# Last stage of a graph-recurrent layer: sums and squares of a block spread over the slots of the blocks before it, lower weights taken from PSUM, PSUM copies on ScalarE

## The reference, cut to what matters

```
xr = h.reshape(b, t * n * d)
mu = xr.mean(axis=0); var = xr.var(axis=0)
xr = (xr - mu) / jnp.sqrt(var + 1e-05) * bn_gamma + bn_beta
h = xr.reshape(b, t, n, d)
lmu = h.mean(axis=(1, 2, 3)); lvar = h.var(axis=(1, 2, 3))      # per row
h = (h - lmu) / jnp.sqrt(lvar + 1e-05) * ln_gamma + ln_beta
scores = jnp.squeeze(h @ attn_w.T + attn_b, -1)
w = jax.nn.softmax(scores, axis=-1)
out = jnp.einsum('btn,btnd->btd', w, h)
```

## Time and profile before

| | us |
|---|---|
| median of 3 runs | 2437.35 (2435.56 to 2440.09) |
| the profiled execution | 2435.1 |
| its span in the trace | 2433.3 |
| TensorE busy in the span | 2279.1 (94%) |
| VectorE, ScalarE, GpSimd busy | 1103.7, 975.1, 135.1 |

### The profile page before, as it was taken

How to read it: one execution, slowest core, us unless ns; L and a number is a source line. 1 busy time by engine, 2 the same in 40 slices (tenths; PEclk the granted TensorE clock), 3 DMA queues, 4 the chain that set the end, 5 groups by cost and what they waited for, 6 DMA issues and landing times. The chain is left out here.

```text
span 2433.3 us, 35457 instructions
## 1 busy us (share of the span) xinstructions
PE 2279.1 (94%) x12462; PEld 1815.6 (75%) x12462; DVE 1103.7 (45%) x2191; ACT 975.1 (40%) x1625; POOL 135.1 (6%) x124
## 2 busy tenths in 40 slices
PE   8999999999999999999999993999999999957787
PEld 7888888888888888888888882887878777832333
DVE  5333223233244332223333222677778777764456
ACT  4322212222233222122222121777778777746340
POOL 0000000000000000000000000111111101004230
PEclk9999999999999999999999996999999999977899
DMA  6321122221253220222220213445455454338430
GB/s 225 122 84 48 69 84 88 88 84 39 75 178 119 85 89 28 86 88 85 87 86 28 88 29 107 129 141 149 142 146 153 139 152 135 111 105 204 128 93 5
DMA packets 137744, 250.97 MB, mean 103 GB/s; under 512 B 11734, under 2 KB 97398, under 8 KB 134390
## 3 DMA queue, kind: packets, MB, share of 16 engines
q1 hardware_dynamic: 119546, 212.59, 28.5%
q10 hardware_dynamic: 18144, 37.69, 4.8%
HBM read 182.54 MB, written 67.70 MB: 103 GB/s over the span
## 5 line engine op out<-in xcount | busy, mean ns | idle before, releaser
L344 PE MATMUL psum<-w_hi,x_lo 128*128 128x500 f32 x2080 | 821.0, 395 | 8.2 <-DVE w_lo L214 8.2
L344 PE MATMUL psum<-w_lo,x_hi 128*128 128x500 f32 (+1 forms) x2080 | 810.3, 390 | 0.0
L344 PE MATMUL psum<-w_hi,x_hi 128*128 128x500 f32 x1920 | 746.1, 389 | 0.0
L278 DVE TENSOR_REDUCE rows<-u 128x10 f32<-128x500 f32 x160 | 107.6, 673 | 919.3 <-ACT u L227 919.1
L344 PEld LDWEIGHTS psum<-w_hi,x_lo 128*128 128x128 f32 x2080 | 391.6, 188 | 83.7 <-issue 8.2
L344 PEld LDWEIGHTS psum<-w_lo,x_hi 128*128 128x128 f32 (+1 forms) x2080 | 392.2, 189 | 75.3
L344 PEld LDWEIGHTS psum<-w_hi,x_hi 128*128 128x128 f32 x1920 | 360.9, 188 | 73.4
L233 ACT COPY at<-psum 128x640 f32<-128x640 f32 x160 | 111.0, 693 | 699.8 <-PE psum L324 699.8
L679 PE MATMUL psum<-adj_sb,xs_sb 100*64 100x100 f32 x2048 | 239.7, 391 | 29.6 <-DMA xs_sb<-xm 29.6
L679 PEld LDWEIGHTS psum<-adj_sb,xs_sb 100*64 100x64 f32 x2048 | 197.8, 219 | 64.3 <-issue 64.3
L227 ACT ACTIVATE u<-psum 128x500 f32<-128x500 f32 x160 | 94.0, 587 | 334.2 <-PE psum L344 334.2
(11 more groups left out here) (162 smaller groups left out, 2319.6 us busy)
## 6 DMA issues: line engine op xcount, KB each, us to landing
w_raw<-W SPq DMA_DIRECT2D x140, 500.0 KB, 6.8
adjT<-at SPq DMA_DIRECT2D x320, 125.0 KB
adj_sb<-adjT SPq DMA_DIRECT2D x16, 2500.0 KB
hF<-hC ACTq DMA_DIRECT2D x96, 256.0 KB, 2.2
h<-hF SPq DMA_DIRECT2D x64, 256.0 KB, 4.6
xs_sb<-xm SPq DMA_DIRECT2D x32, 400.0 KB
xg_sb<-xg ACTq DMA_DIRECT2D x14, 800.0 KB, 13.4
h<-hF SPq DMA_DIRECT2D x48, 192.0 KB, 3.8
```

The source lines that it names most:

```text
L278: nc.vector.tensor_reduce(rows[:, 0], u[:, c2], AX.X, ALU.add).then_inc(dve_step, 1)
L344: last = nc.tensor.matmul(mm_out(w % 2), a[0:r, k, cols], b[0:r, k, :], start=k == 0 and n == 0, stop=k == KF and n == 1)
```

## The change

- `sums_of` of block `i + 1` stands one batch to a slot. Batches 0 to 3 (`EARLY`) of block `i + 2` stand in slots 3 to 6 of block `i`, batches 4 to 6 of block `i + 1` in slots 0 to 2. Ahead of block 0 stand all of block 0 and four batches of block 1. The matmul of `acc` gets its own function, `close_sums`, at the end of slot 2, and `turn_sums` follows the spreads of slot 3.
- The turn of the next block's first weights comes ahead of the last pool batch and of `finish`; the other two kinds are turned in slot 1 instead of slot 0.
- `w_lo` is made from PSUM instead of from `wT`, so it waits for `w_hi` alone; ScalarE copies `wT` 0 later.
- The copies `qs`, `O_sb` and `res` go from VectorE to ScalarE, whose order is written anew.
- `sq` and `sqp` have four buffers instead of three.
- VectorE's woven softmax begins behind the first chunk of slot 3.

The same matmuls, squares, additions and DMAs are made as before.

```diff
+SQ_BUFS = 4
...
-        ahead = lambda i: (5 if i == 0 else 1) if i + 1 < NBLK else 0
-        SUMS_AT = 2
-        POOL_FIRST = batches[SUMS_AT][-1]
+        EARLY = 4
+        POOL_FIRST = batches[QC - EARLY][0]
...
 # VectorE
             def softmax(i):
-                dve.wait_ge(sums_done, i + 1)
-                wait(dve, qt_done, i)
-                V.tensor_copy(qs[:], q_bank).then_inc(qs_ready, 1)
-                yield
                 dve.wait_ge(qt_done, i + 1)
...
-                if i:
-                    result(i - 1)
-                dve.wait_ge(wT_ready, 3 * i + 1)
-                V.tensor_tensor(w_lo[:], wT[:, 0], w_hi[:].bitcast(fp32), ALU.subtract).then_inc(w_lo_ready, 1)
...
-                dve.wait_ge(pr_used, FC * (i + 1))
-                V.tensor_copy(O_sb[:], o_bank).then_inc(o_ready, 1)
...
+            def low_weights(i):
+                dve.wait_ge(w_hi_ready, i + 1)
+                V.tensor_tensor(w_lo[:], wT_bank(0), w_hi[:].bitcast(fp32), ALU.subtract).then_inc(w_lo_ready, 1)
...
             for i in range(NBLK):
+                low_weights(i)
                 pool(i)
-            result(NBLK - 1)
...
 # ScalarE
+            def softmax(i):
+                copy_sums(i)
+                squares(i + 1, 0, 1)
                 act.wait_ge(var_ready, i + 1)
                 nc.scalar.activation(st[:, 7], st[:, 6], ACT.Sqrt, bias=eps[:]).then_inc(rstd_ready, 1)
-                for k in range(first // 2):
-                    square(i + 1, k)
+                squares(i + 1, 2)
                 act.wait_ge(shifted, i + 1)
                 nc.scalar.activation(sc[:, 2, :, 0:TN], sc[:, 1, :, 0:TN], ACT.Exp).then_inc(exp_ready, 1)
-                for k in range(first // 2, first):
-                    square(i + 1, k)
-                copy_weights(i)
+                squares(i + 1, 3)
+                high_weights(i)
+
+            squares(0, *range(QC))
+            softmax(0)
+            for i in range(NBLK):
+                if i:
+                    result(i - 1)
+                copy_weights(i, 0)
+                squares(i + 1, EARLY)
+                copy_weights(i, 1, 2)
+                squares(i + 1, *range(EARLY + 1, QC))
                 if i + 1 < NBLK:
-                    for k in range(first, FC):
-                        square(i + 1, k)
+                    softmax(i + 1)
+                copy_pooled(i)
+            result(NBLK - 1)
...
 # TensorE
+            close_sums(0)
             turn_sums(0)
+            for n in range(EARLY):
+                sums_of(1, n)
+            pe.wait_ge(cols_ready, 2)
+            turn_weights(0, 0)
             for i in range(NBLK):
-                left = list(range(QC)) if i + 1 < NBLK else []
-                while left and left[0] < ahead(i):
-                    sums_of(i + 1, left.pop(0))
-                if i == 0:
-                    pe.wait_ge(cols_ready, 2)
-                turn_weights(i, 0)
                 pe.wait_ge(w_lo_ready, i + 1)
                 for n in range(QC):
                     spread_weights(i, n)
-                    if n == 0:
+                    if n == 1:
                         turn_weights(i, 1)
                         turn_weights(i, 2)
-                    for _ in range(2):
-                        if left:
-                            sums_of(i + 1, left.pop(0))
+                    if n == QC - EARLY and i + 1 < NBLK:
+                        turn_sums(i + 1)
+                    if n < QC - EARLY:
+                        if i + 1 < NBLK:
+                            sums_of(i + 1, EARLY + n)
+                    elif i + 2 < NBLK:
+                        sums_of(i + 2, n - (QC - EARLY))
                     if n:
                         for k in batches[n - 1]:
                             pool_chunk(i, k)
-                    if n == SUMS_AT and i + 1 < NBLK:
-                        assert not left
-                        turn_sums(i + 1)
+                    if n == QC - EARLY - 1 and i + 1 < NBLK:
+                        close_sums(i + 1)
+                if i + 1 < NBLK:
+                    turn_weights(i + 1, 0)
                 for k in batches[QC - 1]:
                     pool_chunk(i, k)
                 finish(i)
```

More of the change, by code:

```diff
@@ L1067, in square, with squares @@
                     g = i * len(on_pool) + on_pool.index(k)
-                    wait(act, sqp_used, g - 2)
-                    nc.scalar.activation(sqp[:, g % 3], h[:, i % 2, c, :], ACT.Square, bias=Csq[:, c:c + 1],
+                    wait(act, sqp_used, g - SQ_BUFS + 1)
+                    nc.scalar.activation(sqp[:, g % SQ_BUFS], h[:, i % 2, c, :], ACT.Square, bias=Csq[:, c:c + 1],
                                          scale=A[:, c:c + 1]).then_inc(sqp_ready, 1)
-            def copy_weights(i):
-                for k in range(3):
+            def squares(i, *which):
+                for n in which if i < NBLK else ():
+                    for k in batches[n]:
+                        square(i, k)
@@ L1075, in copy_weights, with copy_sums, high_weights @@
+            def copy_sums(i):
+                act.wait_ge(sums_done, i + 1)
+                wait(act, qt_done, i)
+                nc.scalar.copy(qs[:], q_bank).then_inc(qs_ready, 1)
+            def high_weights(i):
+                act.wait_ge(wT_done, 3 * i + 1)
+                wait(act, wb_done, FC * i)
+                nc.scalar.copy(w_hi[:], wT_bank(0)).then_inc(w_hi_ready, 1)
+            def copy_weights(i, *which):
+                for k in which:
                     act.wait_ge(wT_done, 3 * i + k + 1)
@@ L1076, in copy_weights, with copy_pooled @@
                     if k == 0:
-                        wait(act, wb_done, FC * i)
-                        wait(act, w_lo_ready, i)
+                        act.wait_ge(w_lo_ready, i + 1)
                         wait(act, res_done, i)
-                        nc.scalar.copy(w_hi[:], wT_bank(k))
                     nc.scalar.copy(wT[:, k], wT_bank(k)).then_inc(wT_ready, 1)
-            for k in range(FC):
-                square(0, k)
-            for i in range(NBLK):
-                first = sum(len(batches[n]) for n in range(ahead(i)))
+            def copy_pooled(i):
+                act.wait_ge(pr_used, FC * (i + 1))
+                wait(act, res_done, i)
+                nc.scalar.copy(O_sb[:], o_bank).then_inc(o_ready, 1)
```

30 lines of the change are left out of this document (15 added, 15 removed).

## The result

| | before | changed |
|---|---|---|
| median of 4 runs each | 2436.45 (2435.05 to 2440.09) | 2406.11 (2400.33 to 2409.12) |
| ratio | 1 | 0.9869, 95% interval 0.985 to 0.9887 |
| profiled execution | 2435.1 | 2409.12 |
| its span | 2433.3 | 2407.3 |

The forecast was 2405. The program is 30.3 us faster by the medians, 26.0 by the two profiled executions. To see where, I cut stage 3 at its first square, its first spread, and the end of each block's result matmuls.

A forecast was written before the change was run, and what follows sets the result against it. Bound: engines taking turns, none full. Gains 7.5 (opening) - 0.2 + 9.3 + 11.9 (blocks 0 to 2) + 2.5 (block 3) = 31.0 us, giving 2404.1 from the profiled execution, 2406.4 from the median; forecast 2405, range 2394 to 2418.

The forecast's parts named there:

- the meetings: Softmax of blocks 0 and 1: GpSimd adds hold up VectorE steps, two to three times a block, 2.0 us.
- Opening: First square to first spread: sums 2.3 us earlier, exponential 2.8, turn of weights 7.0, `w_lo` 0.5; together 7.5 us gained.
- Small parts: Fourth buffer worth 2.3 us in the opening, `w_lo` from PSUM 0.5 us a seam, copies nothing; about 4 us.
- `qs` cost the same on ScalarE: Copies `O_sb`, `res` and `qs` in the blocks: moving them from VectorE changes their cost by at most 0.1 us.
- Block 0: 45.4 us plus 1.4 for first spreads at TensorE's lower level, less 0.5: 46.3 us, 0.2 more than before.
- Blocks 1 and 2: Thinner sums and a shorter seam: 45.4 and 42.8 us instead of 54.74 each, gaining 9.3 and 11.9.
- VectorE's chain of 17.7 less one `pr` is 17.0: Later half of a block, slots 3 to 6: VectorE's work sets the time, 17.0 us, with TensorE's 15.8 hidden.
- rival (a): Blocks 0 to 2: the 2.5 us of waits in slots 0 and 1 vanish, 7.5 less, 2397 us; 18%.
- Rival (b): Softmax of blocks 0 and 1: seven adds each hold a VectorE step 1.04 us, 7.3 a block, 2416 us; 22%.
- Exponential: Later half of a block: it waits 0.6 us behind twelve squares, a square root and two table loads on ScalarE.
- (c): Slots 3 to 6: ScalarE, TensorE and VectorE still take turns, blocks 0 to 2 save nothing, 2425 us; 4%.
- (d): Four blocks: TensorE runs at its lower clock level, adding about 102 us, 2507 us; 2%.

The follow-up runs named there:

- kernel with narrow adds: Changed kernel with GpSimd adding only 8 of the 512 columns of its squares: stage 192.8 us, ratio 0.9818.
- kernel with the small parts: Kernel before with four square buffers, `w_lo` from PSUM, and `qs`, `O_sb`, `res` copied on ScalarE, old order of sums and turns: ratio 0.9961.
- late turn: Changed kernel with the next block's first weight turn behind the result matmuls again, and `w_hi` behind the `O_sb` copy: stage 207.0 us, ratio 0.9884.

## Why the prediction was right, and where it was not

Its order of things was right: what bounds the later half, the wait in slot 1, the seam and the meetings came as told. That the total hit to 0.7 us of the stage is in part luck. The opening gave 3.2 less than forecast, and blocks 0, 1 and 2 gave 2.3, 0.5 and 1.2 more, of which 1.4 by a clock level that block 0 had in some kernels and not in others.

- **Opening, 7.5 forecast, 4.3 measured: the term that failed.** It came short in three places, counted from the first square. *The sums:* `qs` is copied at 25.4 us instead of 26.9, 1.5 earlier where 2.3 was forecast. This is scatter: with four buffers in the kernel before it was 24.6, and 24.5 in two kernels with the changed opening. *The exponential, put at 2232.4 by addition:* from `qs` to its end I had 11.5 us, it took 12.6 (before: 12.0). For more of VectorE's softmax now stood beside GpSimd's adds for block 1: the steps over their usual length sum to 6.2 us, 3.4 before, and ScalarE waited 1.51 for the exponential's input. I had counted meetings in blocks 0 and 1 and none more in the opening; by the kernel with narrow adds they cost 1.5 there. *Behind the exponential:* 7.2 us to the first spread, 5.9 forecast. My prices for four squares and a turn were those of TensorE's higher level; the four transposes took 1.09, and in the kernel without GpSimd's sums, where they took 0.64, it is 5.9. (7.5 less than 2245.82 is 2238.3, not the 2238.4 that I gave for the first spread.)
- **Small parts, 4 forecast, 12.4 alone.** The step "`qs` cost the same on ScalarE" looked at the length of the copy and not at what it queued behind. The row named it (1.51 <- VectorE's `qs`), and the kernel with the small parts shows 1.6 us from it in block 1. The total didn't suffer: in the changed kernel the copy lies off the path in either place, and blocks 0 to 2 were priced as new sums, not as differences.
- **Block 0, 1.4 us too dear by the clock.** Its first spreads were put at the lower level, and in the changed kernel's profile ran at the higher. In three sister kernels (three buffers, late turn, copies on VectorE) they ran at the lower, as forecast, and the way from first spread to turn was 20.0 to 20.2 instead of 18.3. What TensorE did in the 10 us ahead, waits included, was the same to 0.01 us in the kernel with three buffers and in the changed one, so its rows don't tell what decided it; this stays open. In the other kernels with the changed order they ran at the higher level, as in the changed one.
- **Blocks 1 and 2, 45.4 and 42.8 forecast, 45.0 and 41.6 measured.** To the turn of the sums 19.7 was forecast and 18.7 measured; of that, 0.3 is the wait in slot 0 (0.23 instead of 0.5) and 0.15 that in slot 1 (1.85 instead of 2.0), and the rest lies in unit prices a few per cent too high. The later half was 19.76 in block 1 instead of 19.6, but by other terms. The step "VectorE's chain of 17.7 less one `pr` is 17.0" counted things twice: the 17.7 already held the meeting of L979 (0.75) and two waits for TensorE (0.30 and 0.35). Block 2, which has neither, shows 16.1 with the exponential in it, so 15.5 without. On that come, in block 1, about 0.6 at the exponential, 0.8 for the wait for a pool matmul that I had not foreseen, and 2.7 of meetings. Moving the squares of slot 1 took 2.0 off each block: rival (a), that this wait would go by itself, was wrong.
- **Meetings, 2.0 a block forecast, 2.1 and 2.75 measured.** Step by step in block 1, over the lengths of block 2: L964 0.51, L975 1.07, L982 0.21, L1004 0.51, L1007 0.44, which is 2.7, and the narrow adds take just this away. The 2.1 is block 0 of one profile, where L975 was not held; in the kernels with three buffers, with the late turn and with slot 1's squares first its later half is as long as block 1's (19.7 to 19.8). Rival (b), 7.3 a block, was wrong for the blocks; in the opening, where the adds ran nearly back to back, seven steps were held for 6.2, but only 1.5 of it lay on the path. The Trainium skill (SBUF — State Buffer, "Who interferes with whom") has a whole instruction shut out for VectorE steps with two inputs in SBUF. The longest here agrees (L975, 1.69 beside an add of 1.4); but in the blocks only some of the eight were held, since it takes an add and a step at the same moment. Steps over 128x4 values were held as well (L964, 0.67 instead of 0.16).
- **Exponential, 0.6 forecast, 0.60 measured, for a wrong reason.** I had it wait behind twelve squares and the table load. ScalarE was early: it had waited 2.17 to 5.12 us for L994 in blocks 0 to 2. The 0.60 is the exponential itself between two steps that stand next to each other, and a `pr` between them removes it. Block 2, for which I had no wait, shows 0.60 too.
- **Seams, block 3, copies, loads** came as forecast: no wait for `w_lo`, 26.1 against 25.9, copies that weigh nothing, and no wait for a load of `h`.
- Rivals (c) and (d) did not come: no block is over 45.0, and the granted clock of the blocks is 0.96 or more.

## What to carry to other kernels

When a copy moves to another engine, look up what it queued behind and not only how long it takes; and when work is moved beside other engines, count meetings in every stretch where they now overlap, the opening too. Before work is handed to a slow engine to spare TensorE, see whether it would have cost TensorE anything: here a slot with four squares side by side was as long as one with two, and giving two of them away cost 8 us by the meetings and the later sums. Where the part ahead of the change scatters by more than an effect, cut the trace at the change's own first instruction and compare lengths from there.

## What the runs showed of the hardware

- A VectorE step over 128x4 values was held up by GpSimd adds as a large one was: L952 took 1.19 us in the opening and 0.22 elsewhere.
- Four squares at four places of the array, 32 columns each, make a slot no longer than two: 2.72 us from its scores to the next spreads, against 2.71. With two, the pool matmuls at the other places start beside them (2301.33 and 2301.32, kernel with narrow adds).
- In the opening seven steps of VectorE were held for 6.2 us by adds, and the path from `qs` to the exponential was only 1.5 longer for it (12.6 and 11.1).
- The granted clock of one stretch differs between kernels that do the same there, and takes 1.8 to 3.4 us with it: 0.90 or 1.00 from first spread to turn in block 0 (20.1 and 18.3 us), 0.94 or 0.85 in block 1 of the kernel before and of that with the fourth buffer (54.7 and 58.1).
